# Sixteen-head attention among residual rows: ScalarE normalises three groups, VectorE three inside the last two steps

## The reference

```python
x = x + tanh(g_xattn[0]) * L0_xattn(layernorm(x), ctx, ...)        # attn0: linear attention
x = x + tanh(g_ffn[0])   * L0_ffn(layernorm(x), ...)               # ffn0: mixture of experts, top 1
x = x + tanh(g_xattn[1]) * L1_xattn(layernorm(x), ctx, mask, ...)  # attn1: 16 heads, 64 context rows
x = x + tanh(g_ffn[1])   * L1_ffn(layernorm(x), ...)               # ffn1: 8 dense experts, silu gate
x = x + tanh(g_xattn[2]) * L2_xattn(layernorm(x), ctx, mask, ...)  # attn2: one head, tiled
x = x + tanh(g_ffn[2])   * L2_ffn(layernorm(x), ...)               # ffn2: mixture of experts, top 1
x = x + tanh(g_xattn[3]) * L3_xattn(layernorm(x), ctx, mask, ...)  # attn3: 16 heads, 64 context rows
x = x + tanh(g_ffn[3])   * L3_ffn(layernorm(x), ...)               # ffn3: mixture of experts, top 2
```

## Time and profile before

| | |
|---|---|
| median of 3 executions | 2018.11 us (2017.21 to 2020.7) |
| the profiled execution, own time | 2007.31 us |
| its span | 2005.5 us |
| TensorE busy | 1868.8 us, 93% |
| VectorE busy | 1420.0 us, 71% |
| ScalarE busy | 1083.3 us, 54% |
| GpSimd busy | 712.7 us, 36% |
| mean granted TensorE clock | 0.968 |

### The profile page before, as it was taken

One profiled execution on the slowest core, in us unless ns is written; L12 is line 12 of the kernel. 1 busy time (PEld: TensorE's weight loads), 2 busy tenths in 40 slices (PEclk: granted clock), 3 DMA queues, 4 the chain that ended last, 5 costly groups with the idle time before them and its releaser, 6 DMA issues.

```text
span 2005.5 us, 35094 instructions
## 1 busy us (share of the span) xinstructions
PE 1868.8 (93%) x11630; PEld 1573.8 (78%) x11630; DVE 1420.0 (71%) x2404; ACT 1083.3 (54%) x1979; POOL 712.7 (36%) x735
## 2 busy tenths in 40 slices
PE   7989996999999999999999999999998996798993
PEld 4669996777888888888888888888767996686993
DVE  4867776778777777777777777777766664776674
ACT  4348884666555555555555555555424773473771
POOL 3013442464443443543534435434002232252331
PEclk8999998999999999999999999999989998899997
DMA  4056763001100000000001011031105542103554
GB/s 124 1 154 193 205 191 108 2 2 32 32 16 31 31 16 31 31 16 31 17 30 31 16 31 31 16 108 55 44 22 158 146 142 68 41 2 110 171 144 140
DMA packets 113579, 138.96 MB, mean 69 GB/s; under 512 B 15332, under 2 KB 101606, under 8 KB 113504
## 3 DMA queue, kind: packets, MB, share of 16 engines
q1 hardware_dynamic: 105952, 121.70, 20.1%
q0 software_dynamic: 7552, 16.24, 2.9%
HBM read 117.22 MB, written 24.90 MB: 71 GB/s over the span
## 4 chain that ended last, share of the span: by engine, by line
PE 80%; DVE 10%; ACT 4%; issue 3%; DMA 2%; SPq 0%; ACTq 0%; DVEq 0%; POOL 0%; POOLq 0%
PE ps L677 43%; PE ps L936 10%; PE ps L937 10%; PE ps L938 10%; PE ps L684 2%; PE ps L872 1%; ACT ps L1565 1%; DVE xs L1770 1%; ACT wsplit L1526 1%; DVE bn L1683 1%; PE ps L1136 1%; DVE wsplit L2136 1%; DVE lnx L1672 1%; DVE h_lo L2117 1%; ACT h_hi L1569 1%
## 5 line engine op out<-in xcount | busy, mean ns | idle before, releaser
L677 PE MATMUL ps<-h_hi,wsplit 128*128 128x512 f32 (+3 forms) x2016 | 589.2, 350 | 1.8 <-DVE xT L1903 1.3
L677 PEld LDWEIGHTS ps<-h_hi,wsplit 128*128 128x128 f32 x2016 | 367.2, 188 | 48.2 <-DVE xT L1903 1.7
L677 PE MATMUL ps<-h_lo,wsplit 128*128 128x512 f32 (+3 forms) x1008 | 352.4, 350 | 0.0
L563 POOL TENSOR_TENSOR wsplit<-wraw,zero 128x256 fp32r<-128x256 f32 (+2 forms) x160 | 150.9, 960 | 500.8 <-PE ps L938 411.0
L1447 ACT ACTIVATE lnx<-ps 128x512 f32<-128x512 f32 x384 | 229.0, 597 | 107.6 <-PE ps L938 63.8
L677 PE MATMUL ps<-xTh,wsplit 128*128 128x256 f32 (+2 forms) x992 | 254.8, 311 | 8.1 <-DVE h_lo L2117 4.2
L1903 DVE TENSOR_TENSOR xT<-xT,ps 128x1024 f32<-128x1024 f32 x124 | 151.5, 1222 | 121.8 <-PE ps L677 121.8
L1456 ACT ACTIVATE h_act<-h_act 128x512 f32<-128x512 f32 x192 | 120.8, 629 | 207.8 <-DVE h_act L1881 207.7
L1460 ACT ACTIVATE h_hi<-ps 128x512 fp32r<-128x512 f32 x256 | 152.6, 596 | 146.4 <-PE ps L677 145.2
L2117 DVE TENSOR_TENSOR h_lo<-ps,h_hi 128x256 fp32r<-128x256 f32 (+2 forms) x248 | 117.7, 474 | 151.3 <-ACT h_hi L1569 150.3
L1890 DVE TENSOR_TENSOR ps<-h_act,ps 128x512 f32<-128x512 f32 x256 | 177.5, 694 | 44.9 <-PE ps L938 30.9
(11 more groups left out here) (289 smaller groups left out, 3632.0 us busy)
## 6 DMA issues: line engine op xcount, KB each, us to landing
wraw<-in_L_w SPq DMA_DIRECT2D x124, 512.0 KB, 3.9
wraw<-in_L_ffn_Wg SPq DMA_DIRECT2D x32, 256.0 KB, 2.7
wraw<-in_L_ffn_Wu SPq DMA_DIRECT2D x32, 256.0 KB, 3.0
wraw<-in_L_ffn_Wd SPq DMA_DIRECT2D x32, 256.0 KB, 3.6
x_tok<-lnx SPq DMA_DIRECT2D x12, 512.0 KB, 3.9
lnx<-y_tok SPq DMA_DIRECT2D x12, 512.0 KB, 6.1
y_tok<-lnx SPq DMA_DIRECT2D x3, 2048.0 KB, 13.8
wat<-in_attn SPq DMA_DIRECT2D x16, 256.0 KB, 4.9
```

The costliest lines, as they stand in the source:

```text
L563: return pool.tensor_tensor(out_, in_, zero[:, :].to_broadcast(shape), ALU.add)
L677: return pe.matmul(out_, lhsT, rhs, start=start, stop=stop)
```

## The change

In attn1 and attn3:

- ScalarE gets `norm_group`: it normalises groups 0, 1 and 2 as `xs * st_rstd + nmr`. The new small array `nmr` is minus the mean times `st_rstd`, made by VectorE between the rows. VectorE still normalises group 3.
- The moments of a group are made after the first row of the next group instead of after its last.
- The two mask operations stand behind the last moments, so in front of the first `bound`.
- TensorE turns group 1 behind `query(0)` instead of in front of it.
- At the end, VectorE makes the moments of groups 0 to 2 before step 14 and normalises groups 0 and 1 in step 14, group 2 in step 15 and group 3 after the last moments. ScalarE makes the first three `norm_rstd` in step 14, in front of `inverse(14)`. TensorE's 26 fillers behind the last projection are gone.

In ffn2 and ffn3 ScalarE splits two pieces of weights before the turned groups are copied and two behind the last copy of the logits; before the change all four came first.

The core of the diff:

```diff
@@ pe, mha
                 pe.wait_ge(m_tab, 6 * (m + 1))
-                turn_group(n, 1)
...
                 query(0, True)
+                turn_group(n, 1)
+                scores(0, True)
                 turn_group(n, 2)
-                scores(0, True)
                 turn_group(n, 3)
...
                 output(NT - 1)
-                fill(0, 26)
@@ act
+            def norm_group(n, m, g):
+                act.wait_ge(nmr_done, (NG - 1) * m + g + 1)
+                for i in range(g * GROUP, (g + 1) * GROUP):
+                    act.activation(lnx[:, i, :], xs[:, i, :], ACT.Identity, bias=nmr[:, i:i + 1], scale=st_rstd[:, i:i + 1]).then_inc(ln_done, 1)
+
@@ act, mha
-                for g in range(NG):
-                    norm_rstd(n, g)
...
                     if more:
                         exps(i + 1, 1 - j)
+                    if next_norm:
+                        for g in range(NG - 1):
+                            norm_rstd(n + 1, g)
                     inverse(i)
+                norm_rstd(n, 0)
+                norm_group(n, m, 0)
+                norm_rstd(n, 1)
                 copy_group(n, 0)
+                norm_group(n, m, 1)
                 query(0)
+                norm_rstd(n, 2)
                 copy_group(n, 1)
+                norm_group(n, m, 2)
+                norm_rstd(n, 3)
                 copy_group(n, 2)
                 copy_group(n, 3)
                 query(1)
@@ act, moe (ffn2, ffn3)
                     weights_upper(0, 0, 0)
+                    weights_upper(0, 0, 1)
                     norm_rstd(n, NG - 1)
-                    for q in range(1, 4):
-                        weights_upper(0, 0, q)
...
                     copy_logits(layer, n, NG - 1)
+                    for q in range(2, 4):
+                        weights_upper(0, 0, q)
@@ dve, add_rows
                     if i > 0:
                         next_stats(n, i - 1)
+                    if m is not None and g > 0 and i % GROUP == 0:
+                        norm_moments(n + 1, g - 1)
+                    if m is not None and g > 0 and i % GROUP == 2:
+                        four = slice((g - 1) * GROUP, g * GROUP)
+                        dve.wait_ge(std_done, norm_no(n + 1, g - 1) + 1)
+                        dve.scalar_tensor_tensor(out=nmr[:, four], in0=mv[:, four, 0], scalar=-1.0, in1=st_rstd[:, four],
+                                                 op0=ALU.mult, op1=ALU.mult).then_inc(nmr_done, 1)
@@ dve, mha
                     if not first:
                         residual(i - 1)
+                    if norms:
+                        norm_group(n + 1, norms[0])
                     heads(i)
                     if not first:
                         next_stats(n, i - 1)
+                    for g in norms[1:]:
+                        norm_group(n + 1, g)
...
                 norm_moments(n, NG - 1)
-                norm(n)
-                for j in range(2):
-                    bound(j, j)
-                    maxima(j, j)
+                bounds_of_mask()
+                bound(0, 0)
+                dve.wait_ge(ln_done, NT * n + 3 * GROUP)
+                norm_group(n, NG - 1)
+                maxima(0, 0)
+                bound(1, 1)
+                maxima(1, 1)
...
                 step(NT - 3, 1)
-                step(NT - 2, 0, ahead=False)
-                step(NT - 1, 1, ahead=False)
                 for g in range(NG - 1):
                     norm_moments(n + 1, g)
+                step(NT - 2, 0, ahead=False, norms=(0, 1))
+                step(NT - 1, 1, ahead=False, norms=(2,))
                 residual(NT - 1)
                 next_stats(n, NT - 1)
                 norm_moments(n + 1, NG - 1)
+                norm_group(n + 1, NG - 1)
```

More of the change, by code:

```diff
@@ L123, in build @@
         item_expert = sb("item_expert", [P, NT], I32)
+        nmr = sb("nmr", [P, NT])
         r_m, r_s, r_k = (sb(n, [P, NT]) for n in ("r_m", "r_s", "r_k"))
@@ L1395, in inverse, with step @@
                     act.activation(rden[:, :, :], rden[:, :, :], ACT.Exp, scale=-1.0).then_inc(m_rs, 1)
-                def step(i, j, queries=True, more=True):
+                def step(i, j, queries=True, more=True, next_norm=False):
                     if queries:
@@ L1415, in mha @@
                 step(NT - 3, 1)
-                step(NT - 2, 0, queries=False)
+                step(NT - 2, 0, queries=False, next_norm=True)
                 step(NT - 1, 1, queries=False, more=False)
                 if layer == 1:
-                    for g in range(NG):
-                        norm_rstd(n + 1, g)
+                    norm_rstd(n + 1, NG - 1)
             def ffn1(n):
@@ L1765, in _, with add_rows @@
             attn0()
-            def add_rows(layer, n, g):
+            def add_rows(layer, n, g, m):
                 dve.wait_ge(fetched[g], 16 * FETCHED[layer])
@@ L1795, in mha, with bounds_of_mask @@
                                           ALU.add).then_inc(m_kblk, 1)
-                dve.wait_ge(in_mask, 16 * MASKS[layer])
-                if layer == 1:
-                    nb = B
-                    src = mask8[:, 0:B, :]
-                else:
-                    nb = NT
-                    src = mask32[:, :, :]
-                link(dve.tensor_scalar(bmask[:, 0:nb, :], src, 0.0, BIG, ALU.not_equal, ALU.mult))
-                link(dve.tensor_scalar(bmask[:, 0:nb, :], bmask[:, 0:nb, :], MASKED[layer], None, ALU.add))
-                base = NT * m
+                base = NT * m
+                def bounds_of_mask():
+                    dve.wait_ge(in_mask, 16 * MASKS[layer])
+                    if layer == 1:
+                        nb = B
+                        src = mask8[:, 0:B, :]
+                    else:
+                        nb = NT
+                        src = mask32[:, :, :]
+                    link(dve.tensor_scalar(bmask[:, 0:nb, :], src, 0.0, BIG, ALU.not_equal, ALU.mult))
+                    link(dve.tensor_scalar(bmask[:, 0:nb, :], bmask[:, 0:nb, :], MASKED[layer], None, ALU.add))
                 def bound(i, j):
@@ L1826, in residual, with step @@
                                              op0=ALU.mult, op1=ALU.add).then_inc(x_done, 1)
-                def step(i, j, first=False, ahead=True):
+                def step(i, j, first=False, ahead=True, norms=()):
                     if ahead:
@@ L2096, in moe @@
                 nth, cap, items, tiles = MOE.index(layer), CAP[layer], ITEMS[layer], IR[layer] // P
-                if layer:
+                if layer == 2:
                     norm(n)
@@ L2163, in moe @@
                     for g in range(NG):
-                        add_rows(layer, n, g)
+                        add_rows(layer, n, g, None)
             if "ffn0" in N:
```

8 lines of the change are left out of this document (2 added, 6 removed).

## The result

On one chip, 20 executions of each, the changed kernel takes 2023.19 us (2019.14 to 2025.7) and the kernel before 2018.99 us (2015.14 to 2021.7). The ratio is 1.0017, with a 95% interval of 1.0010 to 1.0024: slower by 2 to 5 us.

A forecast was written before the change was run, and what follows sets the result against it. TensorE's own pace was taken as the bound (80% of the chain), leaving four seams: into attn1 +7.2, out +1.6, into attn3 -1.3, out -2.6. Sum +4.9 us on 2018.11 gave 2023.0, range 2014 to 2028.

The forecast's parts named there:

- Into attn1, chain +5.7: Start of attn1: groups 1 and 2 wait for ScalarE's copy of turned group 0, making scores(1) 5.7 us later.
- Clock +1.5 a start, bounds 0 and 3: Starts of attn1 and attn3: TensorE's waits lower its clock, costing 1.5 us each, between 0 and 3.
- Into attn3 -8.5 for the mask: Start of attn3: rows no longer wait for the mask, so the first row starts 8.5 us sooner.
- Out of attn1 +1.6: End of attn1: VectorE's normalisations, held by GpSimd's instructions, delay `heads(15)`; the seam loses 1.6 us.
- the third rival: Clock at its lower level through both starts and attn1's last projection: +9 to +10 us, 2028; chance 0.12.
- The rival in which the normalisations slip through: End of attn1: normalisations slip between GpSimd's instructions, -5.4 us instead of +1.6, total 2013 to 2016; chance 0.15.
- Out of attn3 -2.6: End of attn3: GpSimd is silent and ScalarE's copy follows `norm_rstd(3)` at once, 2.6 us sooner.
- Removed fillers 0: Ends of attn1 and attn3: removing 26 fillers, 3.0 us where TensorE waited for the norm, changes nothing.
- My four seams: Into and out of attn1 and attn3, the only places the change could move: together +4.9 us.

The follow-up runs named there:

- e8: Changed kernel with 6, 18 and 6 filler matmuls in TensorE's waits before turning groups 1, 2 and 3: into attn1 1.2 us shorter, into attn3 3.2.
- e5: Changed kernel with the end of attn1 (moments, four `norm_rstd`, 16 normalisations) put back behind the last step: ratio 1.0000 to the kernel before.
- e7: Changed kernel with the 26 fillers put back behind the last projection in both attentions: ratio 1.0041 to the kernel before.
- e1: Kernel before with only the mask operations moved behind VectorE's 16 normalisations: ratio 0.9962.
- e2: Changed kernel with VectorE's norm, ScalarE's four `norm_rstd` and TensorE's turning order put back at both starts: into attn1 costs 0.1 us instead of 6.8.
- e4: As e3, and VectorE normalises group 3 right behind the last moments, before mask operations and first bound: into attn1 costs 0.6 us instead of 6.8.
- e6: Changed kernel with GpSimd's first ffn1 weight splitting held until VectorE has normalised group 2: `heads(15)` 3.64 us after `heads(14)`, instead of 9.49.
- e11: As e9, with all four weight pieces ahead of the copies of the turned groups: out of attn3 +1.4 us against the kernel before.
- e12: As e1, with two weight pieces ahead of the copies and two behind the logits: out of attn3 -1.1 us against the kernel before.
- e3: Changed kernel with only ScalarE's order changed, normalising its three groups before copying turned group 0: into attn1 costs 2.5 us instead of 6.8.
- e10: As e4, with the end of attn1 as in the kernel before: ratio 0.9931 to the kernel before.
- e9: Changed kernel with both starts' norm on VectorE and the end of attn1 as before, mask behind the norm: ratio 0.9928 to the kernel before.

## Why the prediction was right, step by step

I predicted 2023.0 us, slower the likeliest; measured were 2023.19, or +3.4 (by the ratio) to +4.2 us (by the medians) where I had +4.9. That the medians agree to 0.2 us is partly the base, which is 2018.99 over 20 executions and not the 2018.11 to which I added. The parts:

- **Into attn1, chain +5.7.** +5.5 in e8, without the clock; but of it the way from the first turning to scores(1) is 4.8, where I had 5.3, and the later first turning 0.8, where I had 0.4. Two small misses cancel. The four activations of a group took 2.06 us; I used 2.0. The estimate from the figures of the Trainium skill ("ScalarE: Activation LUTs", section "What ACT_TABLE_LOAD costs") was 2.06 as well: here the page agrees with the trace. In the changed kernel's own trace the first turning came 0.7 late.
- **What I missed there.** VectorE stood 8.01 us in front of `nmr` of group 2, because `norm_rstd(2)` comes late in ScalarE's order, and its last two rows came behind that. It changes little: group 3 then waited only 0.46 us, for the `norm_rstd` that was on my chain anyway.
- **Clock +1.5 a start, bounds 0 and 3.** In the changed kernel's trace 1.2 into attn1 and 3.2 into attn3; in e5 to e7, which start alike, a net against e8 of -0.2 to 0 into attn1 and of -0.5, +4.1 and +4.2 into attn3. That the clock falls after the waits of the turnings was right, and e8, with fillers in these waits, shows that they are the cause. In attn1 the fall covers the last turnings and never the 32 fillers; in attn3 it covers these too in three of four traces, and there it was above my bound of 3: this is the term that I set too low. I also took the 30 fillers as unchanged, but they took 4.77 to 6.12 us in the kernels with the changed start, and with ScalarE's norm that moves the first turning.
- **Into attn3 -8.5 for the mask.** -8.6, in e1 alone. I had the two mask operations hidden; in attn3 they stand with 1.4 us ahead of VectorE's group 3, where attn1's take 0.4, and e8's chain is 0.4 us longer there (13.29 against 12.92). With the chain +5.5 and the clock +3.2 the sum is +0.2 instead of -1.3.
- **Out of attn1 +1.6.** +2.0; `heads(15)` came 9.49 us after `heads(14)`, where my times for them (449.4 and 440.15) gave 9.25. The size is partly luck: the last projection took 2.08 us instead of 1.13 at the lower level, which my sum had at nothing and only the third rival named, and the rest of the way from `heads(15)` to the first copy was some 0.7 shorter than I had carried. In three kernels (e2, e4, e8) the seam is +2.9 to +3.2: the first product stands where the changed kernel's does, but some of the first nine take 0.63 to 0.80 us there, where the changed kernel's take 0.40 to 0.50. The rival in which the normalisations slip through falls with the changed kernel's own rows, and e6 shows the cause. The page "SBUF — State Buffer" of the Trainium skill (section "Who interferes with whom") calls this an exclusive lock held for a whole instruction; the trace agrees, with 5.78 us for four normalisations against 1.37.
- **Out of attn3 -2.6.** -3.0. It needs the pieces behind the logits and the normalisations in the steps; e11 and e12 have one each.
- **Removed fillers 0.** Right against before (e5), but only half the story: left in, they would have cost 1.7 and 1.9 us (e7).
- **ffn1, not in my sum.** -2.0, below. My four seams come to +6.0 in this trace, 1.1 above the 4.9; this gain made up for it. Part of the precision of 2023.0 is therefore luck.

## What to carry to other kernels

Giving an idle engine work helps only where its in-order program lets it start before the thing it is meant to shorten: here one reordering, with no work changed (e3), was worth 4.3 us at one start and 6.1 at the other, the clock's share included. It is no gain by itself: with the order right, ScalarE's groups were no faster than VectorE's norm (e10 against e9). Before VectorE gets work in a stretch where GpSimd runs without gaps, count one normalisation for each GpSimd instruction, long ones included. And test a change of many parts one part at a time: a single moved wait (the mask) was worth 8 us and vanished in a total of +4.

## What had not been expected of the hardware

In every kernel built on the changed code, ffn1's loop is 2.0 us faster, though none of the edits is in it. The last 40 fillers ahead of its long part and its last transpositions, in e1:

```profile
465.24 4.54 PE L684 MATMUL ps<-ident 128*128 128x256 bf16 x40
...
1446.36 1.91 PE L1037 MATMUL ps<-ident,xT 128*128 128x128 f32 x16
```

and in the changed kernel:

```profile
481.18 4.54 PE L686 MATMUL ps<-ident 128*128 128x256 bf16 x40
...
1460.34 1.91 PE L1038 MATMUL ps<-ident,xT 128*128 128x128 f32 x16
```

From the end of the one to the start of the other are 976.58 and 974.62 us. The three kernels with the old code (before, e1, e12) have 976.58 to 976.61, the eleven others 974.51 to 974.68. One of ffn1's 32 units takes 30.73 us in the one and 30.67 in the other, and the difference builds up evenly over the loop. The 26 fillers are not the cause (e7 has them and is fast), nor are TensorE's turning order and ScalarE's norms (e9 has neither changed), nor the order of the pieces (e12 has it and is slow, e11 has it not and is fast). What the eleven share and the three have not is the array `nmr`, its semaphore, and the changed end of attn3. Which of these it is, by the place of other arrays or of the code, was not tried and stays open.
